# Row maxima of a causal attention kept in two halves of heads, one half split by GpSimd

## What is computed

```python
def _L0_attn_ref(in_features, Wq, Wk, Wv, Wo):
    B, S, D, H = (2, 256, 128, 16)
    DH = D // H
    seq_len = in_features.shape[-2]
    q = in_features @ Wq.T
    k = in_features @ Wk.T
    v = in_features @ Wv.T
    q, k, v = (split(q), split(k), split(v))
    scores = jnp.einsum('...hqd,...hkd->...hqk', q, k) / np.sqrt(DH)
    causal = jnp.triu(jnp.ones((seq_len, seq_len), bool), k=1)
    scores = jnp.where(causal, jnp.float32(-1000000000.0), scores)
    weights = jax.nn.softmax(scores, axis=-1)
    out = jnp.einsum('...hqk,...hkd->...hqd', weights, v)
    out = jnp.moveaxis(out, -3, -2).reshape(*in_features.shape[:-1], D)
    return out @ Wo.T

x = x + _L0_attn_ref(_layernorm(x, axis=-1), ...)
```

## Time and profile before

| | |
|---|---|
| median of 3 runs | 617.69 us (614.75 to 617.83) |
| the profiled execution | 615.97 us |
| its span, first to last instruction | 614.2 us |
| attention bodies, first transposition of maxima to the last body's | 35.5 to 278.2 us |
| end of the attention program, start of the experts | about 300 us |

### The profile page before, as it was taken

The page is one execution under the profiler, slowest core; times in us unless marked ns, Lnnn a source line. Parts: engine busy times, 40 slices in busy tenths (PEclk is TensorE's granted clock), DMA queues, the critical chain, the costliest instruction groups (busy, mean ns, idle before and its releaser), DMA issues.

```text
span 614.2 us, 15435 instructions
## 1 busy us (share of the span) xinstructions
PE 532.0 (87%) x5003; PEld 450.9 (73%) x5003; DVE 455.5 (74%) x1307; ACT 365.1 (59%) x987; POOL 338.6 (55%) x465
## 2 busy tenths in 40 slices
PE   2769898999899989997499999998998876889995
PEld 1436666777667767674299999998996654879995
DVE  5646787977888799766497796554898887896662
ACT  2125556866476657554266776665876755756663
POOL 3104444444447663666775777777763844465555
PEclk9999999999899999997689999999898987889998
DMA  4751333333334442407441333332782213544320
GB/s 122 192 152 58 106 106 106 105 105 107 104 96 130 123 122 85 123 21 269 129 101 51 108 92 96 85 86 77 209 326 78 84 52 98 145 149 142 94 68 20
DMA packets 60540, 69.45 MB, mean 113 GB/s; under 512 B 9289, under 2 KB 51985, under 8 KB 58156
## 3 DMA queue, kind: packets, MB, share of 16 engines
q1 hardware_dynamic: 52736, 52.95, 29.7%
q0 software_dynamic: 7168, 14.77, 7.1%
q10 hardware_dynamic: 556, 0.75, 0.5%
HBM read 45.31 MB, written 23.67 MB: 112 GB/s over the span
## 4 chain that ended last, share of the span: by engine, by line
PE 37%; DVE 6%; ACT 2%; DMA 2%; issue 2%; POOL 1%; SPq 1%; DVEq 0%; ACTq 0%; POOLq 0%
PE h_ps_e L1931 15%; PE y_ps_e L1943 15%; PE xT_ps_e L1919 2%; DMA xt_e<-expert_queues 1%; PE h_ps_e L1995 1%; PE h_ps_e L2036 1%; POOL expert_queues L1202 1%; PE l_ps_e L2015 1%; PE h_ps_e L2000 1%; ACT hT_e L1775 1%; ACT L1790 0%; DVE x L1560 0%; DVE xn_e L1589 0%; POOL out_x L1350 0%; PE h_ps_e L1993 0%
## 5 line engine op out<-in xcount | busy, mean ns | idle before, releaser
L665 DVE TENSOR_REDUCE mx<-max_ps 128x2 f32<-128x512 f32 (+1 forms) x192 | 127.3, 687 | 47.9 <-PE max_ps L286 46.0
L1775 ACT ACTIVATE hT_e<-h_ps_e,wb_e 128x128 f32<-128x128 f32 x448 | 122.3, 388 | 27.7 <-PE h_ps_e L1931 26.3
L1931 PE MATMUL h_ps_e<-xT_e,wb_e 128*128 128x128 f32 x896 | 114.8, 283 | 2.7 <-ACT hT_e L1775 1.3
L1943 PE MATMUL y_ps_e<-wb_e,hT_e 128*128 128x128 f32 x896 | 110.9, 278 | 2.9 <-DVE yt_e L1500 2.9
L1931 PEld LDWEIGHTS h_ps_e<-xT_e,wb_e 128*128 128x128 f32 x896 | 109.3, 199 | 4.3 <-issue 2.4
L1943 PEld LDWEIGHTS y_ps_e<-wb_e,hT_e 128*128 128x128 f32 x896 | 106.2, 195 | 3.1 <-DVE yt_e L1500 3.1
L477 ACT ACTIVATE pT<-sc_ps 128x1024 f32<-128x1024 f32 x64 | 65.6, 1024 | 57.7 <-PE sc_ps L314 57.7
L1350 POOL DMA_INDIRECT expert_rows<-yt_e,go_e x72 | 77.8, 1081 | 32.8 <-issue 18.0
L1487 DVE COPY wb_e<-wpack 128x1156 f32 x112 | 82.7, 780 | 9.1 <-issue 5.1
L916 POOL TENSOR_TENSOR turn<-eps 128x1 f32<-128x1 f32 x64 | 12.9, 201 | 135.3 <-ACT pT L477 135.2
L58 POOL DMA_INDIRECT expert_queues<-rxr,rseats x64 | 65.6, 1025 | 19.6 <-issue 17.3
(11 more groups left out here) (299 smaller groups left out, 994.6 us busy)
## 6 DMA issues: line engine op xcount, KB each, us to landing
wpack<-in_wpack SPq DMA_DIRECT2D x2, 4112.0 KB, 15.0
parts_scratch<-parts SPq DMA_DIRECT2D x15, 384.0 KB, 2.5
xt_e<-expert_queues SPq DMA_DIRECT2D x40, 129.0 KB
xt_e<-expert_queues SPq DMA_DIRECT2D x72, 64.5 KB
wpack<-parts_scratch SPq DMA_DIRECT2D x24, 192.0 KB
kst<-parts_scratch SPq DMA_DIRECT2D x24, 192.0 KB
qst<-parts_scratch SPq DMA_DIRECT2D x72, 64.0 KB
wpack<-parts_scratch SPq DMA_DIRECT2D x62, 64.0 KB
```

Source lines behind the costliest of these rows:

```text
L665: nc.vector.reduce_max(mx[:, s, h0:h0 + n], max_ps[:, (k + 1) % 2, :].rearrange("p (h k) -> p h k", h=n), axis=AX.X).then_inc(unit_reduced, 1)
L1775: last = nc.scalar.activation(hT[i % 2][:, s, c, :], h_ps[h_bank(i)][:, s, c * RT:(c + 1) * RT], ACT.Relu, bias=wb[i % 4][:, s, FF + c:FF ...
L1931: last = nc.tensor.matmul(h_ps[h_bank(i)][:, s, c * RT:(c + 1) * RT], wb[i % 4][:, s, c * P:(c + 1) * P], xT[i % 2][:, s * RT:(s + 1) * RT ...
L1943: last = nc.tensor.matmul(y_ps[i % 2][:, s * D:(s + 1) * D], hT[i % 2][:, s, c, :], wb[i % 4][:, s, FF + FC + c * D:FF + FC + (c + 1) * D] ...
```

## The change

The heads are cut in halves of eight. The tiles `mpad`, `mparts`, `mT` and the semaphores from the split to the DMA exist twice. The units of the first six positions now belong to heads 0 to 7 and the last six to heads 8 to 15, each half with two four-head units and then four two-head units. GpSimd splits the first half (`split_first`) between the masks of groups 0 and 1 of the body before; PE transposes it between values 1 and scores 3 of that body, into a bank of `mix_ps`; ACT copies it between exponentials 2 and 3; SP issues its DMA ahead of the second half's. DVE splits the second half where it split everything before. The sign is no longer turned in the split: ACT's copy multiplies by -1. Scores 0 waits for the first half's rows, scores 2 for the second half's. The projection to v also waits for the copy of the first half, since it writes the same bank.

```diff
         def unit_heads(k):
-            return (0, 4 * k, 4) if k < 4 else (1, 2 * (k - 4), 2)
+            h, j = k // 6, k % 6
+            return (0, 8 * h + 4 * j, 4) if j < 2 else (1, 8 * h + 2 * (j - 2), 2)
...
             def project_v(c, r, normed, projected):
+                if counts(c):
+                    pe.wait_ge(mT_ready[0], c + 1)
...
-            def transpose_max(c):
-                pe.wait_ge(mparts_ready, c + 1)
-                out = max_ps[:, 0, :].bitcast(BF16)
+            def transpose_max(c, h):
+                pe.wait_ge(mparts_ready[h], c + 1)
+                if not h:
+                    pe.wait_ge(resid_ready, min(c + LEAD, NSEQ))
+                    if c == 0:
+                        pe.wait_ge(v_ready, 2)
+                out = (max_ps if h else mix_ps)[:, 1 - h, :].bitcast(BF16)
...
             def scores(c, r, u):
                 if u == 0:
-                    pe.wait_ge(mrows_loaded, (c + 1) * 16)
+                    pe.wait_ge(mrows_loaded[0], (c + 1) * 16)
...
+                if u == 2:
+                    pe.wait_ge(mrows_loaded[1], (c + 1) * 16)
...
             def body(b, r, s1=True, s2=True, s4=True):
                 if s4:
-                    transpose_max(b)
+                    transpose_max(b, 1)
...
                 values(b, r, 0)
                 values(b, r, 1)
+                if s2:
+                    transpose_max(b + 1, 0)
                 scores(b, r, 3)
...
-            def copy_mT(c, r):
-                act.wait_ge(mT_done, c + 1)
+            def copy_mT(c, h):
+                act.wait_ge(mT_done[h], c + 1)
                 if counts(c * 16):
-                    act.wait_ge(mrows_loaded, c * 16)
-                nc.scalar.copy(mT[:], max_ps[:, 0, :].bitcast(BF16)[0:NPART * H, 0:S]).then_inc(mT_ready, 1)
+                    act.wait_ge(mrows_loaded[h], c * 16)
+                nc.scalar.mul(mT[h][:], (max_ps if h else mix_ps)[:, 1 - h, :].bitcast(BF16)[0:NPART * HH, 0:S], -1.0).then_inc(mT_ready[h], 1)
...
                 exp(b, 2)
+                if s2:
+                    copy_mT(b + 1, 0)
                 exp(b, 3)
                 if s2:
                     take_v(b + 1, (r + 1) % NB)
-                    copy_mT(b + 1, (r + 1) % NB)
+                    copy_mT(b + 1, 1)
...
+            def split_first(c):
+                m = mx[:, :, 0:HH]
+                pool.wait_ge(unit_reduced, NU * c + 6)
+                pool.wait_ge(mT_done[0], c)
+                nc.gpsimd.tensor_copy(mparts[0][:, :, 0, :], m).then_inc(first_split, 1)
+                pool.wait_ge(first_split, 3 * c - 2)
+                nc.gpsimd.tensor_tensor(mleft[:], m, mparts[0][:, :, 0, :], ALU.subtract).then_inc(first_split, 1)
+                pool.wait_ge(first_split, 3 * c - 1)
+                nc.gpsimd.tensor_copy(mparts[0][:, :, 1, :], mleft[:]).then_inc(first_split, 1)
+                pool.wait_ge(first_split, 3 * c)
+                nc.gpsimd.tensor_tensor(mparts[0][:, :, 2, :], mleft[:], mparts[0][:, :, 1, :], ALU.subtract).then_inc(mparts_ready[0], 1)
...
                 drop_future(b, 0)
+                if s2:
+                    split_first(b + 1)
                 drop_future(b, 1)
...
                 if s2:
-                    load_rows(b + 1, (r + 1) % NB)
+                    load_rows(b + 1, (r + 1) % NB, 0)
+                    load_rows(b + 1, (r + 1) % NB, 1)
```

More of the change, by code:

```diff
@@ L85, in causal_attention @@
         mx = sb("mx", [P, TPS, H], F32)
-        mres = sb("mres", [P, TPS, H], F32)
-        mpad = sb("mpad", [P, TPS, P], BF16)
-        mparts = mpad[:, :, 0:NPART * H].rearrange("p s (a h) -> p s a h", h=H)
-        mT = sb("mT", [NPART * H, S], BF16)
+        HH = H // 2
+        mleft, mres = (sb(n, [P, TPS, HH], F32) for n in ("mleft", "mres"))
+        mpad = [sb(f"mpad{i}", [P, TPS, P], BF16) for i in range(2)]
+        mparts = [m[:, :, 0:NPART * HH].rearrange("p s (a h) -> p s a h", h=HH) for m in mpad]
+        mT = [sb(f"mT{i}", [NPART * HH, S], BF16) for i in range(2)]
         pT = [sb(f"pT{u}", [P, 3 * 512], F32) for u in range(NQ)]
@@ L119, in causal_attention @@
         unit_done, unit_reduced = sem("unit_done"), sem("unit_reduced")
-        msplit, mparts_ready = sem("msplit"), sem("mparts_ready")
-        mT_done, mT_ready, mrows_loaded = sem("mT_done"), sem("mT_ready"), sem("mrows_loaded")
+        first_split = sem("first_split")
+        msplit = [sem(f"msplit{i}") for i in range(2)]
+        mparts_ready, mT_done, mT_ready, mrows_loaded = ([sem(f"{n}{i}") for i in range(2)] for n in ("mparts_ready", "mT_done", "mT_ready", "mrows_loaded"))
         v_done, v_ready = sem("v_done"), sem("v_ready")
@@ L288, in unit @@
                 last.then_inc(unit_done, 1)
-            def transpose_max(c):
-                pe.wait_ge(mparts_ready, c + 1)
-                out = max_ps[:, 0, :].bitcast(BF16)
+            def transpose_max(c, h):
[5 more added lines that the diff above has]
+                out = (max_ps if h else mix_ps)[:, 1 - h, :].bitcast(BF16)
                 for s in range(TPS):
-                    last = nc.tensor.transpose(out[:, s * P:(s + 1) * P], mpad[:, s, :], identb[:])
-                last.then_inc(mT_done, 1)
+                    last = nc.tensor.transpose(out[:, s * P:(s + 1) * P], mpad[h][:, s, :], identb[:])
+                last.then_inc(mT_done[h], 1)
             def scores(c, r, u):
@@ L547, in prologue @@
                 copy_mT(0, 0)
+                copy_mT(0, 1)
             def body(b, r, s1=True, s2=True, s4=True):
@@ L658, in reduce_unit @@
                 dve.wait_ge(unit_done, c * NU + k + 1)
-                if k == 0:
-                    if counts(3 * c):
-                        dve.wait_ge(msplit, 3 * c)
-                    if counts(c):
-                        dve.wait_ge(mparts_ready, c)
+                if k % 6 == 0 and counts(c):
+                    dve.wait_ge(mparts_ready[k // 6], c)
                 s, h0, n = unit_heads(k)
@@ L808, in prologue @@
                 nc.vector.memset(t["eps"][:], EPS).then_inc(eps_ready, 1)
-                nc.vector.memset(mpad[:], 0.0)
+                for m in mpad:
+                    nc.vector.memset(m[:], 0.0)
                 nc.vector.memset(t["nothing"][:], 0.0)
@@ L1027, in prologue @@
                 store_parts(2, 2)
-                load_rows(0, 0)
+                load_rows(0, 0, 0)
+                load_rows(0, 0, 1)
                 load_stack(2, 2)
```

44 lines of the change are left out of this document (25 added, 19 removed).

## The result

The changed kernel takes **610.0 us** (median of four, 608.6 to 614.7) beside 617.8 for the kernel before on the same chip: ratio 0.990, interval 0.986 to 0.994. The forecast of 613.6 had the sign and the range right and the gain too small: 4.1 us forecast, 7.8 and 6.9 measured.

A forecast was written before the change was run, and what follows sets the result against it. Plain, B and C bodies hang on PE, D on DVE, A on ACT and DVE. Terms 1.2 + 1.8 + 1.4 + 0 - 1.8 + 1.6 - 0.1 = 4.1 us, so 613.6 us from 617.69; range 607.5 to 618.5.

The forecast's parts named there:

- a new wait ahead of unit 4: Sign in the changed profile: PE waits 0.3 to 0.5 us for DVE ahead of unit 4.
- Lockstep that takes everything: Rival: in plain, B and C bodies DVE and the last masks absorb all scores 0 gave; 618.0 us, chance 0.24.
- the whole wait that comes back: Rival: all 14.0 us of PE's waits ahead of the scores and body 15's 1.6 are gained; 602.1 us, chance 0.06.
- late behind the store of parts: Rival: SP issues the first half's rows behind that store, which waits for POOL's L911; 619.5 us, chance 0.03.
- the 0.20 at 84.37: Plain bodies: PE's 0.20 us wait for exponential 2 shrinks, in exchange for 0.13 of new transposes ahead of scores 3.
- B and C bodies, 3.2 forecast: Without the row DMA wait each B body gains 0.6 us and each C body 0.45: 1.8 and 1.4 us.
- A bodies, -1.8 forecast: Three bodies hanging on ACT and DVE: first exponential does not move, the split delays values 1, 0.6 us lost each.
- the price of the split: GpSimd's four split instructions, 0.23 us each with three gaps of 0.16: 1.4 us, from 0.5 to 2.7.
- D bodies, 0 forecast: Bodies hanging on DVE: 0.5 us won ahead of unit 4's reduction, set against DVE held up by POOL: 0.
- the charge of 0 to 0.8 for GpSimd's new instructions: D bodies: four short POOL instructions of 0.20 us hold DVE up by 0 to 0.8 us per body.
- Body 15, 1.6 forecast: No units there, so scores 0 waits alone for the DMA, 1.57 us, and later steps follow: 1.6 us gained.
- the clock as a rival for body 7: Rival: the new order spares PE the granted clock of 0.85, up to 2.5 us more; 611.1 us, chance 0.07.

The follow-up runs named there:

- e1_both: Changed kernel, but scores 0 of every body waits again for the maxima rows of both halves; all else kept: 616.96 us, ratio 1.000.
- e3_twice: Changed kernel with GpSimd's four split instructions run twice, first into tiles nobody reads: 615.53 us, ratio 0.998.
- e11_busy15: Changed kernel with nine matmuls that write a bank nobody reads, in PE's idle time in body 15: 610.4 us, ratio 0.987.
- e13_busy_all: Changed kernel with unread matmuls in body 15, the attention's tail and ahead of the experts, and body 3's variances behind the second half's split: 605.5 us, ratio 0.982.

## Why the prediction was right, and where its sizes were off

**Right, by its own steps.** The wait ahead of scores 0 was the lever: with it back the gain is gone (e1_both). In plain bodies the steps came out: scores 0 and unit 4 within 0.04, a new wait ahead of unit 4 (0.22, forecast 0.3 to 0.5), scores 1 earlier by 0.4, scores 2 by 0.3, the body by 0.2 to 0.4. Nearly half of what scores 0 wins is lost to DVE, as it said, and values 1 waits for GpSimd in no body. Lockstep that takes everything (618.0) and the whole wait that comes back (602.1) are both out. The row DMA was not late behind the store of parts: no body's scores 0 waits for it.

**What was luck.** The total lies inside a range of 11 us, but the gain was put at little more than half. Of the 3.2 us between the two sums of the table, 1.5 come from the D bodies, by a mechanism that no term stands for, 1.0 from body 15, where the clock came on top of the wait, and 1.6 from the A bodies, mostly because the split was priced too high; the plain, B and C bodies gave 0.9 less than forecast.

**Two readings of the trace were off.** The 14.0 us are not all the wait that the change takes away: 2.8 of them are the 0.20 ahead of scores 3, so the whole wait was worth at most 11.2 and not 14.0. And the 0.20 at 84.37 is no wait for exponential 2, as that row names none; it did not shrink but moved to the new transposes. From scores 2 to scores 3 body 2 takes 0.13 more than before, just the price put on the two transposes, which is why 0.23 and not 0.3 is left at its end.

**B and C bodies, 3.2 forecast, 2.5 measured.** Up to scores 1 the assumption held that the transposes of router rows behind unit 4 let more of the gain through: in body 5 scores 1 starts 0.63 earlier, in body 2 0.40, after the same wait of 0.22 ahead of unit 4. What the prediction charged in body 2 and left out here came behind that, the longer unit 7 and the new transposes: 0.51 is left at scores 2, 0.38 at scores 3 and 0.39 at the end of body 5, where 0.6 had been taken.

**A bodies, -1.8 forecast, -0.2 measured.** The failed term is the price of the split, 1.4 us for 1.06, by the gap between dependent instructions. Put into the prediction's own sum, 1.06 - 0.54 - 0.4 + 0.13 is 0.25 a body, and 0 to 0.14 was measured. e3_twice bears the sum out in kind: with no cover left, one more split of 1.0 us cost these bodies 1.3 each.

**D bodies, 0 forecast, 1.5 measured.** The mechanism was seen on one instruction only. DVE instructions with two SBUF inputs wait for GpSimd's masks too, not only for L911, and the earlier scores move the masks out of their way. Body 7 before, then after (DVE):

```profile
156.66 0.59 DVE L755 TENSOR_TENSOR rcand<-rlg,top 128x48 f32<-128x48 f32 x1
...
158.36 0.58 DVE L767 TENSOR_TENSOR rpick<-rcand,rcmax 128x48 bf16<-128x48 f32 x1
```

```profile
156.96 0.21 DVE L773 TENSOR_TENSOR rcand<-rlg,top 128x48 f32<-128x48 f32 x1
...
157.81 0.20 DVE L777 TENSOR_TENSOR rcand<-rcand,cst 128x48 f32<-128x48 f32 x1
...
158.27 0.21 DVE L785 TENSOR_TENSOR rpick<-rcand,rcmax 128x48 bf16<-128x48 f32 x1
...
161.82 0.52 DVE L777 TENSOR_TENSOR rcand<-rcand,cst 128x48 f32<-128x48 f32 x1
...
162.61 0.86 DVE L797 TENSOR_TENSOR rpick<-rcand,rcmax 128x48 bf16<-128x48 f32 x1
```

0.59, 0.58 and the 1.09 of the earlier trace rows became 0.21, 0.21 and 0.52; the last of the pick went the other way, 0.86 (L797) for 0.46 (L779 before). That it is the early scores 0 that do this, and not GpSimd's split, e1_both shows: it has the split and the old wait, and its body 7 has the old times again, 1.0 us longer at the full clock (DVE):

```profile
156.41 0.59 DVE L774 TENSOR_TENSOR rcand<-rlg,top 128x48 f32<-128x48 f32 x1
...
158.12 0.69 DVE L786 TENSOR_TENSOR rpick<-rcand,rcmax 128x48 bf16<-128x48 f32 x1
...
161.91 1.09 DVE L778 TENSOR_TENSOR rcand<-rcand,cst 128x48 f32<-128x48 f32 x1
```

And the charge of 0 to 0.8 for GpSimd's new instructions was not due: L777 took its 0.20 at 157.81, although GpSimd began the last instruction of the split while it ran. The rule drawn from the Trainium skill in the prediction (GPSIMD Engine Reference, section Key points: GpSimd contends with VectorE instructions that have two SBUF inputs) agrees with these rows in kind. The rows add the size: in body 7 before, each of these instructions that was held up had started while a mask or L911 ran, and it ended 0.06 to 0.07 us after GpSimd's. In body 7 after none started within a short instruction of the split, so whether those would hold DVE up is not shown.

**Body 15, 1.6 forecast, 2.6 measured.** The term for the wait was right, about 1.5 (above). What came on top, 1.1 here, is the clock, 0.2 to 1.7 us from one execution to the next. The prediction had the clock as a rival for body 7 and not here, where the wait stood in the trace beside a granted clock of 0.78.

**Body 7's clock** was spared in both profiles of the changed kernel, but also in e1_both, which has the wait, and body 4 or 11 had low stretches instead. So the rival's 2.5 us are not shown to be a gain of the change.

## To carry to other kernels

A wait in front of two engines that go in step is not worth its length: here the nine plain, B and C bodies lost 7.1 us of PE's time to it and gained 3.5, the slack of the engine behind. Where nothing else fills the engine, as in body 15, it was worth its whole length, and the clock gave more on top. Short work is best put on the engine that idles anyway, but its cover has an end: here one more split of the same length took back most of the gain, and it went first in the bodies with the least idle time. When a change shifts one engine by a fraction of a microsecond, look at every instruction of its neighbour that was seen to wait for it (here DVE's with two inputs in SBUF, beside GpSimd's masks), since such collisions come and go with the shift.

## What the runs showed of the hardware

- **TensorE's clock differs between executions of one kernel.** The same idle time was followed by a stretch at half clock in some executions and not in others. PE idles 1.2 us ahead of body 4's transposes (1.26 in the kernel before); of nine profiles with early scores and body 3 unchanged seven had a stretch at 0.5 in body 4 of 3.4 to 10.2 us, which made the body 1.5 to 3.7 us longer. None of the two with the wait had one, and none of the two with the variances moved. Whether the earlier scores bring it on is not settled by so few, and it would be a cost of the change that the prediction did not have. The first profile against e11_busy15, body 4:

```profile
104.34:121.77 17.43, 16.87 (x162) 12.50 (x165) 14.12 (x38) 12.67 (x23) 7.38 (x17) 0.80 0.31 92
```

```profile
104.75:123.83 19.08, 18.35 (x163) 13.50 (x165) 14.37 (x38) 12.77 (x23) 7.35 (x17) 0.73 0.28 85
```

- **Matmuls that nobody reads can pay** where PE would idle: in the profile of e13_busy_all, with 26 of them, the granted clock was 1.00 over 27 us that had run at 0.74, which gave 1.2 us. In two of its six runs the clock over the whole run was no higher than without them.
- **GpSimd passes from one dependent short instruction to the next in 0.06 to 0.08 us** (0.28 from start to start for 0.20 to 0.22 of work on 16 columns), a third of the gap that the one place in the trace before had shown.
